# The last head of two attention stages: scores in pairs of neighbouring PSUM banks, one exponential for two

## The reference, cut to what matters

```
q = x @ Wq; k = x @ Wk; v = x @ Wv                # 8 columns of each belong to the head
scores = q @ k.T / sqrt(8)                        # 2048 x 2048 per head
weights = softmax(scores, axis=-1)                # layer 3: only keys at or before the query
out = weights @ v
```

## Time and profile before

| what | value |
|---|---|
| median of 3 runs | 1891.17 us (1891.07 to 1896.22) |
| profiled execution, its own time | 1891.83 us |
| its span, first to last instruction | 1890.1 us |
| TensorE busy | 1628.9 us, 86% |
| VectorE busy | 1425.7 us, 75% |
| ScalarE busy | 1113.8 us, 59% |
| GpSimd busy | 337.4 us, 18% |
| exponentials of the heads (L880) | 1664, 819.4 us busy |
| mean granted TensorE clock | 0.929 of 2.4 GHz |

### The profile page before, as it was taken

How to read it: one execution, slowest core, us unless ns; L and a number is a source line. 1 busy time by engine, 2 the same in 40 slices (tenths; PEclk the granted TensorE clock), 3 DMA queues, 4 the chain that set the end, 5 groups by cost and what they waited for, 6 DMA issues and landing times. The chain is left out here.

```text
span 1890.1 us, 28648 instructions
## 1 busy us (share of the span) xinstructions
PE 1628.9 (86%) x9625; PEld 632.9 (33%) x9625; DVE 1425.7 (75%) x2696; ACT 1113.8 (59%) x2266; POOL 337.4 (18%) x628
## 2 busy tenths in 40 slices
PE   2789999999999996779997798895549999999987
PEld 1422222222222222434444444684222222222246
DVE  5689999999999963675555606565768999999925
ACT  3158888888888884232222243454214777777754
POOL 0101200001000000000000334553012333312133
PEclk8879999999999998799998899998657999999999
DMA  4101211111110011115333259963430111111132
GB/s 124 49 21 48 75 61 52 48 66 63 58 47 30 23 24 31 67 41 121 94 93 126 94 158 307 298 220 83 156 93 28 50 50 50 49 46 56 37 85 71
DMA packets 76117, 155.62 MB, mean 82 GB/s; under 512 B 16312, under 2 KB 33592, under 8 KB 72276
## 3 DMA queue, kind: packets, MB, share of 16 engines
q1 hardware_dynamic: 64250, 125.63, 21.0%
q0 software_dynamic: 11504, 27.62, 4.7%
q10 hardware_dynamic: 218, 0.55, 0.1%
HBM read 103.41 MB, written 48.89 MB: 81 GB/s over the span
## 5 line engine op out<-in xcount | busy, mean ns | idle before, releaser
L880 ACT ACTIVATE heads_probs<-heads_pS 128x512 f32<-128x512 f32 (+3 forms) x1664 | 819.4, 579 | 169.7 <-PE heads_pS L795 167.7
L904 DVE TENSOR_REDUCE heads_run_max<-heads_pM 128x1 f32<-128x1024 f32 x512 | 600.7, 1219 | 28.5 <-PE heads_pM L771 19.6
L811 PE MATMUL heads_pO<-heads_probs,heads_vh 128*32 128x512 f32 (+2 forms) x3328 | 446.0, 583 | 0.8 <-ACT heads_probs L880 0.7
L771 PE MATMUL heads_pM<-heads_ks,heads_qs 56*128 56x512 bf16 (+3 forms) x1040 | 317.6, 380 | 23.2 <-DVE heads_run_max L915 8.5
L795 PE MATMUL heads_pS<-heads_qs,heads_ks 59*128 59x512 bf16 (+3 forms) x1040 | 292.6, 368 | 0.8 <-ACT heads_probs L880 0.8
L915 DVE TENSOR_REDUCE heads_run_max<-heads_pM 128x1 f32<-128x512 f32 x384 | 246.5, 683 | 7.1 <-PE heads_pM L771 7.1
L771 PE MATMUL heads_pM<-heads_k_first,heads_q_first 56*128 56x512 bf16 x624 | 191.0, 383 | 31.6 <-DVE heads_run_max L944 15.3
L795 PE MATMUL heads_pS<-heads_q_first,heads_k_first 59*128 59x512 bf16 x624 | 180.1, 378 | 4.6 <-ACT heads_probs L880 4.6
L795 PEld LDWEIGHTS heads_pS<-heads_qs,heads_ks 59*128 59x128 bf16 x1040 | 76.7, 93 | 267.3 <-ACT heads_probs L880 232.4
L912 DVE CUSTOM_DVE_ANT_0 heads_masked_out<-heads_pM,heads_mask_end 128x128 bf16<-128x128 f32 (+3 forms) x256 | 121.1, 486 | 11.0 <-PE heads_pM L771 8.5
L1431 ACT ACTIVATE top_act_gate<-top_pG 128x512 f32<-128x512 f32 x68 | 40.6, 597 | 136.9 <-PE top_pU L1387 136.9
(11 more groups left out here) (379 smaller groups left out, 1963.8 us busy)
## 6 DMA issues: line engine op xcount, KB each, us to landing
top_weights<-k_comb_dram SPq DMA_DIRECT2D x128, 128.0 KB, 3.0
second_w<-in_L_W_dram SPq DMA_DIRECT2D x12, 1024.0 KB, 11.5
k_hid_slots_dram<-k_zeros SPq DMA_DIRECT2D x8, 1152.0 KB, 4.4
k_h_slots_dram<-second_work SPq DMA_DIRECT2D x48, 192.0 KB, 2.9
second_work<-k_hid_slots_dram SPq DMA_DIRECT2D x48, 192.0 KB, 3.5
heads_qs<-k_parts_dram SPq DMA_DIRECT2D x40, 192.0 KB
heads_ks<-k_parts_dram SPq DMA_DIRECT2D x80, 96.0 KB
k_parts_dram<-proj_part SPq DMA_DIRECT2D x12, 512.0 KB, 4.1
```

Of the source, the lines that this page charges most:

```text
L771: mm = pe.matmul(pM[:, bank_of(c, j, k), 0:w], qs[c % ROUND][rows, i * P:(i + 1) * P], ks[c % ROUND][rows, b * BLK:b * BLK + w], start=Tru ...
L811: mm = pe.matmul(pO[k * 32:k * 32 + VW, o:BLK], vh[c][:, t, at:at + VW], probs[u % 2][:, k * BLK + o:(k + 1) * BLK], start=first_chunk[u] ...
L880: act.activation(probs[u % 2][:, k * BLK + c0 - b * BLK:(k + 1) * BLK], pS[:, slot, 0:c1 - c0], ACT.Exp)\
L904: dve.reduce_max(run_max[:, i, blocks[0][0] // 2:blocks[0][0] // 2 + 1], both.rearrange("p k c -> p (k c)"), AX.X).then_inc(taken, 2)
```

## The change

For the last head (LAST = 15) alone:

- Scores go to *pairs* of neighbouring banks, in turn to three pairs (WIDE). Layer 0: banks 0 and 1 of `pM`, banks 2 and 3 of `pM`, banks 0 and 1 of `pS`. Layer 3: banks 0 and 1 of `pM`, 0 and 1 of `pS`, 2 and 3 of `pS`. The even chunk goes to the first bank of its pair and the odd to the second, each at its own column offset, so that a full odd chunk begins where the even one ends.
- `score_last` waits at chunk 0 for the rows of maxima and for all maxima to be reduced (`pM` is then free), at the first pair in `pS` for all exponentials of head 14, and from the fourth pair on, at the even chunk only, for the exponential of the pair three before.
- From unit 1 of the last head on, what stands after the sums of unit u is the four chunks of unit u+2 in both layers (AHEAD = 4); in layer 0 the five chunks 7 to 11 stand after the sums of unit 0.
- ScalarE waits for both scores of a pair and then takes one exponential over both banks, up to 1024 columns. Where the odd chunk has an offset of its own (four pairs in layer 3) it takes two. The pair counts two on `exped`. In layer 0 the copy of head 14's sums stands after the first pair.
- Layer 0: 64 exponentials become 32. Layer 3: 40 become 24.

```diff
--- before.py
+++ after.py
@@ -602,6 +602,18 @@
 
             return n + (1 if n >= TURN_AT and exists(p, c + 1) else 0)
 
+        LAST = HEADS - 1
+        WIDE = [(pM, 0), (pS, 0), (pS, 2)] if causal else [(pM, 0), (pM, 2), (pS, 0)]
+        AHEAD = 4
+
+        def wide_banks(n):
+
+            bank, at = WIDE[n // 2 % len(WIDE)]
+            return bank[:, at:at + 2, :].rearrange("p k c -> p (k c)")
+
+        def offset(n):
+            return chunks[n][4] - chunks[n][3] * BLK
+
         def load_stacks(p, c):
 
             h = ROUND * p + c
@@ -632,8 +644,6 @@
                 queue.dma_start(K.head_more[h, :, (b - 2) * BLK:(b - 1) * BLK], ot[c][k * 32 + SHIFT:k * 32 + SHIFT + HD + 1, :])\
                      .then_inc(stored, 16)
 
-
-        LAST = HEADS - 1
 
         def store_last(queue, turn):
             queue.wait_ge(ot_kept, LAST + 2)
@@ -795,6 +805,22 @@
                 pe.matmul(pS[:, slot, 0:c1 - c0], ks[c % ROUND][rows, u * P:(u + 1) * P], qs[c % ROUND][rows, c0:c1],
                           start=True, stop=True).then_inc(scored, 1)
 
+            def score_last(p, c, n):
+
+                _, _, u, _, c0, c1, _ = chunks[n]
+                if n == 0:
+                    pe.wait_ge(rows_in, 16 * PARTS * HEADS)
+                    pe.wait_ge(taken, BLOCKS * HEADS)
+                if n % 2 == 0:
+                    if n >= 2 * len(WIDE):
+                        pe.wait_ge(exped, EVENTS * LAST + n - 2 * len(WIDE) + 3)
+                    elif WIDE[n // 2][0] is pS:
+                        pe.wait_ge(exped, EVENTS * LAST + 1)
+                rows = slice(0, STK + PARTS)
+                out = wide_banks(n)[:, n % 2 * BLK + offset(n):(n % 2 + 1) * BLK]
+                pe.matmul(out, ks[c % ROUND][rows, u * P:(u + 1) * P], qs[c % ROUND][rows, c0:c1], start=True, stop=True)\
+                  .then_inc(scored, 1)
+
             def sum_unit(p, c, u):
 
                 h = ROUND * p + c
@@ -816,7 +842,9 @@
             def one_head(p, c):
                 for u in range(NU):
                     sum_unit(p, c, u)
-                    new = [(c + n // NC, n % NC) for n in range(first_chunk[u + 1] + RING, first_chunk[u + 2] + RING)]
+                    last = ROUND * p + c == LAST
+                    new = [(c + n // NC, n % NC) for n in range(first_chunk[u + 1] + (AHEAD if last and u > 0 else RING),
+                                                                first_chunk[u + 2] + (AHEAD if last else RING))]
                     new = [(d, n) for d, n in new if exists(p, d)]
                     todo = [(c + d, j) for d, j in ahead(u) if exists(p, c + d)]
                     if causal:
@@ -832,7 +860,7 @@
                             d, n = new[k]
                             if d == c and n == TURN_AT and exists(p, c + 1):
                                 turn(p, c + 1, (EVENTS * (ROUND * p + c) + TURN_AT + 1, (EVENTS * (ROUND * p + c) + TURN_AT + 1) % RING))
-                            score_chunk(p, d, n)
+                            (score_last if ROUND * p + d == LAST else score_chunk)(p, d, n)
 
             AT_ONCE = 3
             for m in range(AT_ONCE if feed else 0):
@@ -865,8 +893,25 @@
                 act.wait_ge(used, NU * (h + 1) + 2)
                 act.activation(ot[h % ROUND][:, :], pO[:, :], ACT.Copy).then_inc(ot_kept, 1)
 
+            def last_head():
+
+                for n in range(0, NC, 2):
+                    u, k = chunks[n][:2]
+                    if not causal and n == 2:
+                        keep_sums(LAST - 1)
+                    act.wait_ge(scored, EVENTS * LAST + n + 3)
+                    if k == 0:
+                        act.wait_ge(used, NU * LAST + u + 1)
+                    whole = [(offset(n), 2 * BLK)] if offset(n + 1) == 0 else [(offset(n), BLK), (BLK + offset(n + 1), 2 * BLK)]
+                    for c0, c1 in whole:
+                        act.activation(probs[u % 2][:, k * BLK + c0:k * BLK + c1], wide_banks(n)[:, c0:c1], ACT.Exp)\
+                           .then_inc(exped, 2 // len(whole))
+
             def one_head(p, c):
                 h = ROUND * p + c
+                if h == LAST:
+                    last_head()
+                    return
                 for n, (u, k, _, b, c0, c1, _) in enumerate(chunks):
 
                     if not causal and n == RING and h > 0:
```

## The result

The changed kernel takes 1883.05 us (median of 5, 1881.61 to 1884.80) against 1891.17 us (median of 5, 1890.57 to 1896.22): the ratio is 0.9947 with a 95% interval of 0.9928 to 0.9966. The span of the profiled execution went from 1890.1 to 1881.7 us. That is 8.4 us, half as much again as the 5.67 forecast. The first question is therefore not whether the change works, but how much of the 8.4 us belongs to it.

A forecast was written before the change was run, and what follows sets the result against it. Layer 0's last head was taken as bound by a closed round of TensorE and ScalarE, layer 3's by TensorE. Layer 0's -6.07 and layer 3's +0.4 us took 1891.17 to 1885.5 us, range about 1882.8 to 1889.0.

The forecast's parts named there:

- The closed round: Layer 0's last head before the change: exponential, sums, scores and ScalarE's wait follow each other, 2.39 us per unit.
- TensorE's own 1.96 us: Last head: TensorE's time for four full scores and a sum without a wait, forecast as layer 0's new unit time.
- The wide exponential: Last heads: one exponential over 1024 columns takes 1.04 us and the next starts after 0.92; bounds 0.87 and 1.11 us.
- Layer 0, -6.07 us: Layer 0's last head: with the round open, the last unit's sums start at 729.27 instead of 735.34 us.
- S0: Start of the sums of unit 0 in layer 0's last head: forecast 699.60 us, before 699.81.
- S1: Start of unit 1's sums in layer 0's last head, behind a half-filled pair: forecast 702.10 us, before 702.20.
- Layer 3, +0.4 us: Layer 3's last head: masks wait for the whole pair's exponential, so the last sums come later; ends +0.2 and +0.6.
- The sum: Whole kernel: -6.07 and +0.4 us make -5.67 against the median, 1885.5 us, at chance 0.70.
- How the numbers follow: Chances for the whole kernel: faster 0.49, within 0.3% 0.47, slower 0.04; also derives the range.
- The clock rival: After layer 0, clock rises move: 2 us earlier at two places, 1883.5 us (0.13); 5 us later, 1888.0 (0.08).
- A failed rise: The full-clock stretch after 766.60 stays at half clock, adding 12.6 us: 1898.1 us; chance 0.04.
- a dear wide read: Last heads: wide exponentials start only every 1.11 us, so ScalarE bounds at 2.22 us per unit: 1890.9 us; chance 0.04.

## Why the prediction was right and wrong, point by point

- *The closed round and TensorE's own 1.96 us:* right, to the hundredth, in every unit from 2 to 14. The wide exponential was taken at 1.04 us and 0.92 between starts; it is 1.02 and 0.92, and no border of a bank shows.
- *Layer 0, -6.07 us:* -5.86. The terms that were a little small: S0 came 2.79 us after head 14's last sums and not 2.70, since a head's first sums start 0.14 us after their exponential (698.75 to 698.89), where 0.05 was taken from the end of a head; S1 came 2.56 after S0 instead of 2.50.
- *Layer 3, +0.4 us:* +0.42, of which the mechanism named, the mask behind the wide read, is 0.32; the remaining 0.1 is not in the working, so that the closeness of the two numbers is in part luck. Unit 8's sums came 0.23 us later than before and not 0.12. GpSimd's release of the sums takes 0.14 us (1809.47 to 1809.62), near the upper end 0.15 of its bounds, not 0.06.
- *The sum:* 5.67 us forecast, 5.44 in the change's own stretches. This is shown in three profiles of the changed kernel, one from each set in which it ran.
- *The total and the range:* here the prediction failed. The ratio 0.9947 puts the changed kernel at 1881.1 us, below the range's 1882.8, though the median of 1883.05 lies in it; and 0.49 for faster by more than 0.3% was too hesitant for what was measured, though not for what the change's own stretches are worth (0.29%). The step that failed is the one that adds up what lies behind the two last heads: there everything was taken to "move with it", and in "How the numbers follow" only the clock, with 2 us, could change it. In the two profiles 2.95 of the 8.38 us come from stretches with no edit in them, and 1.86 and 1.51 of this from the last stage and from layer 3's heads 0 to 14. The runs show two things in its place. First, the last stage does not just move: its fourth tile comes 1.64 us sooner after layer 3's last sums, and the six profiles with layer 3's change have it 1.5 us sooner in the mean than the seven without, with no overlap between the two groups. Second, stretches that the change doesn't touch vary by more than that from one execution to the next: layer 3's heads 0 to 14 took 361.0 to 365.7 us in the thirteen profiles, and the kernel before by itself ran from 1890.57 to 1896.22 us. Nothing in the range stood for either. How the 3 us divide between the two is not known.
- *The clock rival:* right that the shift moves the clock's rises, not that an earlier rise gives time back. Stretches of layer 1's attention after the change, and of the kernel before in its second profile (columns as in the earlier trace rows):

```profile
753.70:758.50 4.80, 4.80 (x15) 3.13 (x16) 3.77 (x15) 1.19 (x2) 0.00 (x0) 0.50 1.00 420
758.60:772.10 13.50, 12.62 (x73) 8.89 (x72) 2.77 (x4) 6.12 (x10) 0.00 (x0) 1.00 0.01 4
```

```profile
759.80:765.80 6.00, 6.00 (x16) 3.56 (x17) 3.79 (x15) 1.79 (x3) 0.00 (x0) 0.50 0.83 345
766.00:779.40 13.40, 12.53 (x77) 9.29 (x75) 2.77 (x4) 5.55 (x9) 0.00 (x0) 1.00 0.00 1
```

  The full clock begins 4.8 us after the stage's first matmul instead of 6.1, and ends as much sooner; the stage takes 77.93 to 77.98 us in the six profiles in which layer 0's stretch is 5.6 to 5.9 us shorter, and 77.08 to 77.63 in the three without a change in layer 0. But the size of the shift isn't what counts: two pairs, 3.4 us earlier, take 77.36 us, and the kernels with six single banks, 6.4 to 6.8 us earlier, take 77.45 to 77.56. The place of the rise orders all thirteen: at 6.2, 6.1, 6.0, 5.9, 5.8 and 5.7 us after the first matmul the stage takes 77.08, 77.28, 77.36, 77.45, 77.52 to 77.56 and 77.63, and at 4.8 to 5.4 us 77.93 to 77.98. The Trainium skill's page "TensorE: Matmul & The Clock Gate", section "What's actually happening", says that the activity is measured freely and not restarted with the work; the trace agrees in so far as the rise stands at 4.8, 5.4 and 5.3 us in three profiles of one kernel. That the clock is the cause of the 0.3 to 0.9 us is argued from this order, not tested.
- *A failed rise, a dear wide read:* neither was there.

**What stays open.** The three ratios of the change are 0.9947, 0.9975 and 0.9956, and its stretches alone would give 0.9971. With 1.5 us less at the start of the last stage and 0.6 us more in layer 1 it would be 0.9966, an estimate from the stretches above. The kernel before against itself gave 0.9988, with an interval that holds 1, so leans of 0.1% appear without a change. Two things aren't settled by these runs: whether the sooner start of the last stage reaches the end of the kernel on every chip, and whether the instruction packet is what moves it.

## What to carry to other kernels

When an engine waits 0.3 us per round and the round closes over two engines, count the banks before the instructions: six banks instead of three, with the scores queued to fit, gave 5.6 us here and merging the reads 0.3, and two pairs of banks kept hardly more than half. Merging reads makes every consumer of the first part wait for the second, so look for who reads a part only (the mask of a diagonal, a half-filled pair) and leave those split. And judge a change of a few us by the stretch that holds it: here the stretch repeated to 0.01 us between chips while totals of one kernel spread over 5 to 15. Then lay the stretches behind it side by side in every kernel that was run, with and without the edit: what comes with the edit each time has to be counted with it, however far behind it stands.

## What the runs showed that was not expected

- One program, different chips: the kernel before took 1891 and 1945 us, and nearly all of the difference lies in the stretch of layer 2 (310.8 against 357.6 us), with the same instructions and the granted clock in layer 0's last head full on both. Over the thirteen profiles that stretch takes 309 to 312 us in six and 358 to 366 in seven, and nothing between.
- The first head of layer 3 has more than one length: 27.07 us from its unit 0 to head 1's in the profile before, 25.37 in the changed kernel's and in the kernel before, again; in the thirteen profiles it is 25.4 us five times, 26.7 to 26.9 six times and 27.1 twice. It makes 1.7 us of difference between executions with no edit near it.
- Sums that follow an exponential start 0.05 us after it at the end of a head and 0.14 us after it at a head's beginning, and 0.14 us after GpSimd's mask.
- A load of 64 KB landed in 2.0 to 2.4 us or in 3.3 to 4.2, and the longer time went with a 16 KB packet of instructions between its issue and its landing, in seven traces of thirteen. All seven are kernels without the edit in the head stage of layer 3, just before.
